# A retention layer and an FP4 feed-forward in one kernel: the old state read in two halves of 64 rows, the output projection behind the gate's projection, the gate product between the rotation's steps

## The chip, the cores and the metric

The kernel runs on one core of a Trainium2 chip. A core has TensorE (PE, matrix products; its weight loads are listed apart as PEld), VectorE (DVE), ScalarE (ACT), GpSimd (POOL) and a queue for DMAs (SP). Each works through its own list of instructions in order, and semaphores connect them. PE writes its results to PSUM, which has eight banks of 2 KB (512 fp32 numbers) in each of 128 partitions; DVE and ACT read them there. The metric is the device time of one execution in microseconds (us).

## What is computed

Input is x of shape (2, 2048, 256). First a retention layer (8 heads, 32 numbers of q and k and 64 of v in each), then a feed-forward whose activations and weights are rounded to FP4 in blocks of 16; behind both a residual and a layer norm.

```python
qkv = x @ w_qkv.T; q, k = xpos(q, k)            # a rotation by position
retention = einsum('bhtd,bhsd->bhts', q, k) * HD_QK**-0.5 * decay_mask   # causal, decay[h]**(t-s)
out = einsum('bhts,bhsv->bhtv', retention, v)
normed = (out - mean) / sqrt(var + eps)         # per head
y = (silu(x @ w_gated.T) * normed) @ w_proj.T
x = layernorm(x + y)
gate, up = fp4_linear(x, w_gate), fp4_linear(x, w_up)
x = layernorm(x + fp4_linear(silu(gate) * up, w_down))
```

The retention is computed in chunks of 128 positions: inside a chunk by scores, and what earlier chunks contribute by a running state of 32 x 64 per head, which decays from chunk to chunk.

## The kernel before

There are 32 tiles (16 chunks of 128 positions, two batches b that alternate, so tile n belongs to batch n % 2). All 32 go through the retention stage, with their results kept on the chip; then all go through the feed-forward. Every engine has a function `body(n, b, piece)` that writes out what it does around tile n of the first stage, and `both_loops` (L252) calls it: tiles -2 to 5 unrolled, tiles 6 to 29 in a loop of 12 rounds of two tiles (b = 0, then b = 1), tiles 30 and 31 unrolled. In the loop each round also quantises one piece of the feed-forward's weights (`w_max` to `w_exponent` on DVE, a rounding on ACT and three steps on POOL); the tile with b = 1 also quantises two finished tiles of x (`x_scale` to `x_exponent`). I call the tiles with b = 0 even and those with b = 1 odd.

There is no scheduler: the order of the calls in `body` is the order on the engine. For tile n it is

- PE (L1273): transposes of the rotated q and k (`turn_qk`, L1210), the projection of q and k of tile n+1 (L1178 into wide_banks), scores (L1221), transposes of the gated tile n-3 (L1261), the update of the state (`update`, L1250), the read of the old state (`cross`, L1230), the projection of v of tile n+1, the product of scores and v (`mix`, L1237), the output projection of tile n-3 (`project_out`, L1178 into upd_y), the projection of the gate of tile n+1 (`project_gate`).
- DVE (L804): the even tile has the root of nine variances as a chain of small steps (L675 to L720, its last result rstd at L715), the odd one the quantising. Both have `decay_q` (L617), `decay_scores` (L625), `split_gated` (L996), `sum_state` (L662), the rotation of tile n+1 (`rotate_products` L598 and L599, `rotate_sum` L609 and L610), in the even tile `w_max` (L759), then the gate product (`apply_gate`, L642), the residual of tile n-3 (`add_resid`, L632), its statistics (L636), the sums of squares (L648).
- ACT (L460): copies and activations; towards the end of a tile the eight scalings of the heads of tile n-2 (`normalise_heads`, L442), in the odd tile a rounding step of x (L404), a copy of v of tile n+1 (L424) and the squares of tile n (`square_heads`, L434).

`mixed`, one bank of 512 columns, takes first cross and then, added to it, mix. `cross` has two matmuls per tile, one per group of four heads: 128 rows of decayed q (4 heads x 32) against a block-diagonal state of 128 x 256, three quarters of it zero. Another bank, `upd_y`, holds the result of `update` (128 columns) and y, the result of `project_out` (256 columns).

`square_heads` reads mixed on ACT and `apply_gate` reads it on DVE; L639 makes DVE wait for the squares, so that the two don't read the bank together. `project_out` waits for `state_summed` of tile n (L1269), since DVE reads upd in y's bank. `add_resid` waits for `y_done`.

The semaphores that matter below: `squared` (ACT L434 to DVE L642), `opened_ready` (from L642), `y_done` (from project_out to DVE L632), `rot_ready` (from L610 to turn_qk), `ret_ready` (from L625 to the projection of v), `rstd_ready` (from L715 to ACT L442), and the step counter of the weights' quantising (from L778 to ACT L409).

## Time and profile before

| | us |
|---|---|
| median of three runs | 651.88 |
| lowest, highest | 650.33, 652.59 |
| the profiled execution | 651.12 |
| its span, first to last instruction | 649.3 |
| PE busy in the span | 583.6 (90%) |
| DVE busy | 552.7 (85%) |
| ACT busy | 337.6 (52%) |
| POOL busy | 230.9 (36%) |

The retention stage fills the span up to some 380 us, the feed-forward the rest. The loop over tiles 6 to 29 runs from about 95 to 354 us. Times in the trace's rows are microseconds from the start of the span. A busy PE is not a PE at its peak: matmuls are pipelined, their durations overlap, and so what a block of matmuls takes is read from its start to the start of the next block. On DVE and ACT too an instruction can start some 0.1 us before the one ahead of it has ended.

### The profile page before, as it was taken

What the parts mean: (1) busy time and instruction counts of PE and PEld (TensorE: products, weight loads), DVE (VectorE), ACT (ScalarE), POOL (GpSimd) and SP (SyncE); (2) the same over time, 40 slices, a digit from 0 to 9 for tenths busy, and PEclk for the clock granted to TensorE, in tenths of its full rate; (3) what the DMA queues carried; (4) which work ended last, traced back from release to release, by engine and by line L of the source; (5) the groups of instructions that cost most, each with busy time, mean ns of one, the idle gap of its engine ahead of it and who ended that gap; (6) DMA issues with size and microseconds to landing.
All of it is one profiled execution on the core that took longest, in us unless ns stands there. A gap on an engine that the chain in (4) does not pass through costs nothing. (4 is left out here: it accounts for less than half of the span.)

```text
span 649.3 us, 14685 instructions
## 1 busy us (share of the span) xinstructions
PE 583.6 (90%) x4290; PEld 498.6 (77%) x4290; DVE 552.7 (85%) x1439; ACT 337.6 (52%) x869; POOL 230.9 (36%) x262
## 2 busy tenths in 40 slices
PE   3269999999999999999999967786999999999975
PEld 2158888888888888888888856676999888888864
DVE  6047779999999999999999767887999999999996
ACT  3124666666756675667565654423454435444333
POOL 1011122344234523452344023435444444444430
PEclk9679999999999999999999979797999999999998
DMA  6471011101110111011101000000000000000001
GB/s 160 56 231 49 11 50 50 40 8 48 48 40 8 48 48 40 8 48 48 40 8 40 11 8 9 1 1 17 16 16 16 16 16 24 24 16 16 17 16 50
DMA packets 25853, 23.11 MB, mean 36 GB/s; under 512 B 2024, under 2 KB 22760, under 8 KB 25832
## 3 DMA queue, kind: packets, MB, share of 16 engines
q1 hardware_dynamic: 25016, 21.27, 11.6%
q10 hardware_dynamic: 816, 1.57, 0.7%
q8 instruction: 11, 0.18, 0.1%
q14 instruction: 10, 0.08, 0.0%
HBM read 17.56 MB, written 5.28 MB: 35 GB/s over the span
## 5 line engine op out<-in xcount | busy, mean ns | idle before, releaser
L1178 PE MATMUL wide_banks<-win_hi,x_hi 128*128 128x512 f32 x192 | 68.8, 440 | 12.9 <-DVE win_lo L882 11.0
L1154 POOL TENSOR_TENSOR shared<-shared,h_scale 128x704 f32<-128x704 bf16 x32 | 44.4, 1388 | 92.0 <-DVE shared L802 92.0
L1178 PE MATMUL wide_banks<-wgu_hi,xq_hi 128*128 128x512 f32 (+1 forms) x192 | 63.4, 413 | 10.6 <-DVE xq_lo L979 10.6
L442 ACT ACTIVATE shared<-opened,rstd 128x64 f32<-128x64 f32 x256 | 64.7, 335 | 11.4 <-DVE rstd L715 11.1
L413 ACT ACTIVATE shared<-shared 128x704 bf16<-128x704 f32 x32 | 25.3, 792 | 81.0 <-POOL shared L1149 81.0
L1237 PEld LDWEIGHTS mixed<-shared 128*128 128x128 f32 x512 | 62.0, 192 | 2.8
L1100 POOL TENSOR_TENSOR kd<-shared 128x128 f32<-128x128 f32 x60 | 23.2, 407 | 111.1 <-DVE shared L610 87.8
L1149 POOL TENSOR_TENSOR shared<-shared,h_inv 128x704 f32<-128x704 f32 x32 | 44.5, 1391 | 50.7 <-DVE h_inv L793 50.7
L1178 PE MATMUL wide_banks<-win_lo,x_hi 128*128 128x512 f32 x192 | 61.3, 401 | 0.0
L1178 PE MATMUL wide_banks<-win_hi,x_lo 128*128 128x512 f32 x192 | 60.9, 398 | 0.0
L1237 PE MATMUL mixed<-shared 128*128 128x64 f32 x512 | 60.6, 271 | 0.0
L1178 PE MATMUL wide_banks<-wgu_lo,xq_hi 128*128 128x512 f32 (+1 forms) x192 | 58.7, 388 | 0.0
L1178 PE MATMUL wide_banks<-wgu_hi,xq_lo 128*128 128x512 f32 (+1 forms) x192 | 57.7, 382 | 0.0
L1115 POOL TENSOR_TENSOR x_lo<-xf,x_hi 128x256 fp32r<-128x256 f32 x32 | 24.3, 758 | 87.5 <-ACT x_hi L394 87.5
L419 ACT ACTIVATE qkT<-turn 128x512 f32<-128x512 f32 x32 | 19.1, 598 | 57.6 <-PE turn L1210 57.6
L1178 PEld LDWEIGHTS wide_banks<-win_hi,x_hi 128*128 128x128 f32 x192 | 31.3, 194 | 19.6 <-issue 18.4
L1178 PEld LDWEIGHTS wide_banks<-wgu_hi,xq_hi 128*128 128x128 f32 x192 | 32.8, 198 | 15.2 <-DVE xq_lo L979 11.8
L1178 PEld LDWEIGHTS wide_banks<-win_lo,x_hi 128*128 128x128 f32 x192 | 37.1, 193 | 8.7
L1178 PEld LDWEIGHTS wide_banks<-win_hi,x_lo 128*128 128x128 f32 x192 | 36.6, 190 | 8.9
L625 DVE TENSOR_TENSOR shared<-wide_banks,shared 128x1024 f32<-128x1024 f32 x32 | 39.0, 1218 | 4.1 <-PE wide_banks L1221 4.1
L1178 PEld LDWEIGHTS wide_banks<-wgu_lo,xq_hi 128*128 128x128 f32 x192 | 37.2, 197 | 6.4
L1178 PEld LDWEIGHTS wide_banks<-wgu_hi,xq_lo 128*128 128x128 f32 x192 | 36.7, 193 | 6.3
(147 smaller groups left out, 1487.8 us busy)
## 6 DMA issues: line engine op xcount, KB each, us to landing
xf<-in_x_feat SPq DMA_DIRECT2D x32, 128.0 KB, 2.3
tab<-in_tables SPq DMA_DIRECT2D x16, 256.0 KB, 2.7
xt<-in_x_tok SPq DMA_DIRECT2D x32, 128.0 KB, 2.1
out<-shared SPq DMA_DIRECT2D x32, 128.0 KB, 1.7
x<-in_w_in ACTq DMA_DIRECT2D x3, 512.0 KB, 5.3
w<-in_w_gu SPq DMA_DIRECT2D x1, 1408.0 KB, 7.7
pow_dram<-powers SPq DMA_DIRECT2D x1, 1056.0 KB
w<-in_w_down SPq DMA_DIRECT2D x1, 704.0 KB, 9.0
```

The lines of the kernel that those rows point to most:

```text
L413: act.activation(h_size[:, b], h_unit[:, b], ACT.Abs, scale=SIZE_BY).then_inc(h_fp4["rounder_ready"], 1)
L419: act.activation(qkT[:].rearrange("p c t -> p (c t)"), turn[:], ACT.Copy).then_inc(qkT_ready, 1)
L442: last = act.activation(gated[:, b, cols], opened[:, b, cols], ACT.Copy, scale=rstd[:, b, 1 + k:2 + k])
L625: dve.tensor_tensor(ret[:].rearrange("p (j g) t -> p j (g t)", g=GROUPS), row_scores, dmask[:].rearrange("p (j g) t -> p j (g t)", g=GROUP ...
L1100: last = pool.tensor_tensor(kd[:, P * g:P * (g + 1)].rearrange("p (j d) -> p j d", d=DQ), rot[:, b, QK + P * g:QK + P * (g + 1)].rearrange ...
L1115: pool.tensor_tensor(x_lo[:, b], xf[:, b], x_hi[:, b].bitcast(F32), ALU.subtract).then_inc(x_lo_ready, 1)
L1149: pool.tensor_tensor(over_blocks(h_unit[:, b]), over_blocks(h), spread(h_fp4["inv"][:]), ALU.mult).then_inc(h_fp4["step"], 1)
L1154: pool.tensor_tensor(over_blocks(hq[:, b]), over_blocks(h_steps[:, b]), spread(h_fp4["scale"][:, b]), ALU.mult).then_inc(h_fp4["ready"], 1)
L1178: last = pe.matmul(dst, lhs, rhs, start=k == 0, stop=k == len(parts) - 1)
L1237: last = pe.matmul(mixed[:, DV * k:DV * (k + 1)], ret[:, slot(k)], vs[:, b, DV * k:DV * (k + 1)], start=False, stop=k == HEADS - 1, skip_g ...
```

## The change

Four things are changed together.

1. `cross` is split by rows: instead of two matmuls of 128 rows x 256 columns there are four of 64 rows x 128 columns. Rows 0 to 63 (heads j = 0, 1 of each group) write to one bank, rows 64 to 127 (j = 2, 3) to another. The block-diagonal state is 128 columns wide instead of 256. `mixed` is now the upper 256 columns of each of two banks, `mixed_banks`.
2. What was upd_y moves into the lower 256 columns of the same two banks: y into bank 0, upd into bank 1. Since banks are now shared otherwise, waits change: `update` and `project_out` wait for the gate product that read mixed (`opened_ready`), `cross` waits for `resid_done`, `mix` waits for `state_summed`. The signal that the update is done is given by `cross`, which stands behind it.
3. On PE `project_out` stands behind `project_gate` instead of ahead of it.
4. On DVE the gate product moves ahead: in the even tile between the second product of the rotation and its sums, in the odd tile between the first and the second product.

The heads' order in mixed, in the gate product and in the rows of w_proj is changed to suit (w_proj is loaded by two DMAs instead of one).

```diff
+def place(h):
+    g, j = divmod(h, PER)
+    return PER * (j // 2) + 2 * g + j % 2
...
-        mixed = psum("mixed", [P, BANK])
-        upd_y = psum("upd_y", [P, GROUPS * DV + DM])
-        upd = upd_y[:, 0:GROUPS * DV].rearrange("p (g v) -> p g v", v=DV)
-        y = upd_y[:, GROUPS * DV:]
+        mixed_banks = psum("mixed_banks", [P, 2, BANK])
+        mixed = mixed_banks[:, :, DM:BANK]
+        y = mixed_banks[:, 0, 0:DM]
+        upd = mixed_banks[:, 1, 0:GROUPS * DV].rearrange("p (g v) -> p g v", v=DV)
...
@@ the DMAs @@
-            sp.dma_start(wproj[:], w_proj.rearrange("(c p) n -> p c n", p=P)).then_inc(ld_proj, 16)
+            for r in range(2):
+                sp.dma_start(wproj[:, 2 * r:2 * r + 2], w_proj.rearrange("(g r p) n -> r p g n", g=GROUPS, p=P)[r]).then_inc(ld_proj, 16)
...
@@ ACT @@
-                act.activation(squares[:], mixed[:], ACT.Square, scale=DV ** -0.5).then_inc(squared, 1)
+                act.activation(halves(squares[:]), mixed, ACT.Square, scale=DV ** -0.5).then_inc(squared, 1)
...
-                    last = act.activation(state_bd[rows, b, :, DV * j:DV * (j + 1)], state[rows, b], ACT.Copy)
+                    last = act.activation(state_bd[rows, b, :, DV * (j % 2):DV * (j % 2 + 1)], state[rows, b], ACT.Copy)
...
@@ DVE @@
-                dve.tensor_tensor(opened[:, b], mixed[:], gate[:, b], ALU.mult).then_inc(opened_ready, 1)
+                dve.tensor_tensor(opened[:, b].rearrange("p (r g c) -> p r g c", r=2, g=GROUPS), mixed.rearrange("p r (g c) -> p r g c", g=GROUPS),
+                                  gate[:, b].rearrange("p (g r c) -> p r g c", g=GROUPS, r=2), ALU.mult).then_inc(opened_ready, 1)
...
                 if valid(n + 1):
-                    rotate_products(n + 1, 1 - b)
+                    rotate_cos(n + 1, 1 - b)
+                    if b == 0:
+                        rotate_sin(n + 1)
+                if valid(n):
+                    apply_gate(n, b)
+                if valid(n + 1):
+                    if b == 1:
+                        rotate_sin(n + 1)
                     rotate_sum(n + 1, 1 - b)
                 if w and b == 0:
                     w_max(piece)
-                if valid(n):
-                    apply_gate(n, b)
...
@@ PE, cross, mix, update, project_out @@
                 need(pe, opened_ready, n)
+                need(pe, resid_done, n - LAG)
                 for g in range(GROUPS):
-                    pe.matmul(mixed[:, PER * DV * g:PER * DV * (g + 1)], qdT[:, g], state_bd[:, b, g],
-                              start=g == 0, stop=False, skip_group_check=True)
+                    for r in range(2):
+                        rows = slice(2 * DQ * r, 2 * DQ * (r + 1))
+                        last = pe.matmul(mixed[:, r, 2 * DV * g:2 * DV * (g + 1)], qdT[rows, g], state_bd[rows, b, g],
+                                         start=g == 0, stop=False, skip_group_check=True)
+                if carried(n):
+                    last.then_inc(upd_done, 1)
...
                 pe.wait_ge(ret_ready, n + 1)
+                if carried(n):
+                    pe.wait_ge(state_summed, n + 1)
                 for k in range(HEADS):
...
-                need(pe, resid_done, n - LAG)
+                need(pe, opened_ready, n)
...
-                pe.wait_ge(state_summed, n + LAG + 1 if not isinstance(n, int) else min(n + LAG + 1, TILES - BATCH))
+                pe.wait_ge(opened_ready, n + LAG + 1 if not isinstance(n, int) else min(n + LAG + 1, TILES))
...
@@ PE, body @@
+                if valid(n + 1):
+                    project_gate(n + 1, 1 - b)
                 if in_turn(n - LAG):
                     project_out(n - LAG)
-                if valid(n + 1):
-                    project_gate(n + 1, 1 - b)
```

`project_out` is called with n - 3, so its new wait asks for the gate product of the tile whose mix stands just ahead of it.

How the orders read on the engines. PE of the kernel before, from mix to turn_qk of the next tile, with the semaphores that each first instruction waits for:

```order
L1237 MATMUL mixed<-shared 128x64 [waits ret_ready]
L1237 MATMUL mixed<-shared 128x64 x7
L1178 MATMUL upd_y<-wproj_hi,gatedT_hi 128x256 [waits state_summed,resid_done,gatedT_lo_ready]
L1178 MATMUL upd_y<-wproj_hi,gatedT_hi 128x256 x3
L1178 MATMUL upd_y<-wproj_lo,gatedT_hi 128x256 x4
L1178 MATMUL upd_y<-wproj_hi,gatedT_lo 128x256 x4
L1178 MATMUL wide_banks<-win_hi,x_hi 128x512 [waits ret_ready,gate_ready]
```

The same place in the changed kernel (L1264 is mix, L1197 is both projections, L1229 turn_qk):

```order
L1264 MATMUL mixed_banks<-shared 128x64 [waits state_summed,ret_ready]
L1264 MATMUL mixed_banks<-shared 128x64 x7
L1197 MATMUL wide_banks<-win_hi,x_hi 128x512 [waits ret_ready,gate_ready]
L1197 MATMUL wide_banks<-win_hi,x_hi 128x512
L1197 MATMUL wide_banks<-win_lo,x_hi 128x512 x2
L1197 MATMUL wide_banks<-win_hi,x_lo 128x512 x2
L1197 MATMUL mixed_banks<-wproj_hi,gatedT_hi 128x256 [waits opened_ready,resid_done,gatedT_lo_ready]
L1197 MATMUL mixed_banks<-wproj_hi,gatedT_hi 128x256 x3
L1197 MATMUL mixed_banks<-wproj_lo,gatedT_hi 128x256 x4
L1197 MATMUL mixed_banks<-wproj_hi,gatedT_lo 128x256 x4
L1229 MATMUL turn<-ident,shared 128x128 [waits gatedT_lo_ready,rot_ready]
```

The output projection has gone behind the gate's, and waits for the gate product of the same tile instead of the state's sum.

DVE in the loop's even tile, from the last steps of the roots to the residual, before:

```order
L715 SCALAR_TENSOR_TENSOR rstd<-poly,fine 128x18
L720 SCALAR_TENSOR_TENSOR shift<-moments,rstd 128x2
...
L598 TENSOR_TENSOR qk_cos<-wide_banks,tab 128x512
L599 TENSOR_TENSOR wide_banks<-wide_banks,tab 128x512
L609 TENSOR_TENSOR shared<-qk_cos,wide_banks 128x16x16
L610 TENSOR_TENSOR shared<-qk_cos,wide_banks 128x16x16
...
L759 TENSOR_REDUCE w_amax<-w 128x22
L642 TENSOR_TENSOR opened<-mixed,shared 128x512
...
L632 TENSOR_TENSOR resid<-upd_y,xt 128x256
```

and in the changed kernel (all line numbers are 10 to 14 higher there; L655 is the gate product, L645 the residual):

```order
L729 SCALAR_TENSOR_TENSOR rstd<-poly,fine 128x18
L734 SCALAR_TENSOR_TENSOR shift<-moments,rstd 128x2
...
L608 TENSOR_TENSOR qk_cos<-wide_banks,tab 128x512
L612 TENSOR_TENSOR wide_banks<-wide_banks,tab 128x512
L655 TENSOR_TENSOR opened<-mixed_banks,shared 128x512
L622 TENSOR_TENSOR shared<-qk_cos,wide_banks 128x16x16
L623 TENSOR_TENSOR shared<-qk_cos,wide_banks 128x16x16
...
L773 TENSOR_REDUCE w_amax<-w 128x22
...
L645 TENSOR_TENSOR resid<-mixed_banks,xt 128x256
```

The gate product has gone ahead of three instructions.

DVE in the odd tile of the changed kernel, with the waits:

```order
L766 TENSOR_SCALAR x_rounder<-x_unit 128x512 [waits x_step]
...
L608 TENSOR_TENSOR qk_cos<-wide_banks,tab 128x512 [waits rot_ready,ld_tab]
L655 TENSOR_TENSOR opened<-mixed_banks,shared 128x512 [waits gated_ready,gate_ready,squared]
L612 TENSOR_TENSOR wide_banks<-wide_banks,tab 128x512
L622 TENSOR_TENSOR shared<-qk_cos,wide_banks 128x16x16 [waits turned,kd_ready,sin_done,cos_done]
L623 TENSOR_TENSOR shared<-qk_cos,wide_banks 128x16x16
L643 ISA [waits y_done]
L645 TENSOR_TENSOR resid<-mixed_banks,xt 128x256 [waits x1_ready,ld_xt0]
```

Before, the gate product (L642, with the same waits) stood between L610 and the wait for y_done; three instructions of the rotation are now behind it. The order on ACT is as it was.

## Rows read from the trace of the kernel before

**Rows 1.** Engines between 100 and 200 us: busy us (instructions), clock, DMA; then waits.
```profile
100.00:200.00 100.00, 99.00 (x830) 82.27 (x830) 93.24 (x232) 66.18 (x191) 38.20 (x50) 1.00 0.13 40
...
PEld turn L1261 <- issue: 2.3, 12, 0.2
DVE opened L642 <- ACT squares L434: 1.9, 2, 1.2
```

**Rows 2.** Timeline of PE: start, us, engine, line, what; mix of an even tile onwards.
```profile
165.82 1.89 PE L1237 MATMUL mixed<-shared 128*128 128x64 f32 x16
167.52 0.71 PE L1178 MATMUL upd_y<-wproj_hi,gatedT_hi 128*128 128x256 f32 x4
...
169.02 0.62 PE L1178 MATMUL wide_banks<-win_hi,x_hi 128*128 128x512 f32 x2
...
170.42 0.60 PE L1210 MATMUL turn<-ident,shared 128*128 128x128 f32 x4
...
181.44 0.60 PE L1210 MATMUL turn<-ident,shared 128*128 128x128 f32 x4
```

**Rows 3.** Timeline of DVE in the same even tile.
```profile
161.93 0.75 DVE L694 SCALAR_TENSOR_TENSOR fine<-rsq,root 128x18 f32<-128x18 f32 x1
...
165.51 0.18 DVE L715 SCALAR_TENSOR_TENSOR rstd<-poly,fine 128x18 f32<-128x18 f32 x1 [0.20 <-DVE poly L709]
...
166.67 0.69 DVE L599 TENSOR_TENSOR wide_banks<-wide_banks,tab 128x512 f32<-128x512 f32 x1
...
168.12 0.51 DVE L759 TENSOR_REDUCE w_amax<-w 128x22 f32 x1
...
168.74 0.69 DVE L642 TENSOR_TENSOR opened<-mixed,shared 128x512 f32<-128x512 f32 x1
...
169.41 0.42 DVE L632 TENSOR_TENSOR resid<-upd_y,xt 128x256 f32<-128x256 f32 x1
```

**Rows 4.** Timeline of ACT in the same even tile.
```profile
165.72 2.02 ACT L442 ACTIVATE shared<-opened,rstd 128x64 f32<-128x64 f32 x8 [0.71 <-DVE rstd L715]
...
168.13 0.58 ACT L434 ACTIVATE squares<-mixed 128x512 f32<-128x512 f32 x1
```

**Rows 5.** Timeline of DVE, PE and ACT in the odd tile that follows.
```profile
173.74 0.34 DVE L778 TENSOR_SCALAR w_rounder<-w_unit 128x352 uint32<-128x352 uint32 x1
174.00 1.22 DVE L625 TENSOR_TENSOR shared<-wide_banks,shared 128x1024 f32<-128x1024 f32 x1
...
174.11 0.50 ACT L409 ACTIVATE w_rounder<-w_rounder 128x352 f32<-128x352 f32 x1 [1.67 <-DVE w_rounder L778]
...
175.36 0.70 PE L1178 MATMUL wide_banks<-win_hi,x_hi 128*128 128x512 f32 x2 [0.15 <-DVE shared L625]
...
178.05 0.68 DVE L598 TENSOR_TENSOR qk_cos<-wide_banks,tab 128x512 f32<-128x512 f32 x1
...
179.23 0.59 ACT L434 ACTIVATE squares<-mixed 128x512 f32<-128x512 f32 x1
...
180.09 0.69 DVE L642 TENSOR_TENSOR opened<-mixed,shared 128x512 f32<-128x512 f32 x1
...
180.69 0.41 DVE L632 TENSOR_TENSOR resid<-upd_y,xt 128x256 f32<-128x256 f32 x1
```

**Rows 6.** One tile's scores and cross: durations in ns, first and last start in us.
```profile
L1221 PE MATMUL wide_banks<-qkT x16: 270/270/372, 183.4 to 183.9; 32*128 32x128 f32 x16
...
L1230 PE MATMUL mixed<-shared,qdT x4: 379/379/483, 185.0 to 185.8; 128*128 128x256 f32 x4
```

**Rows 7.** Timeline of the first tiles: gate product and turn_qk; output projection, gate product, residual.
```profile
53.97 0.69 DVE L642 TENSOR_TENSOR opened<-mixed,shared 128x512 f32<-128x512 f32 x1 [1.75 <-ACT squares L434]
...
54.59 0.60 PE L1210 MATMUL turn<-ident,shared 128*128 128x128 f32 x4
...
71.03 0.72 PE L1178 MATMUL upd_y<-wproj_hi,gatedT_hi 128*128 128x256 f32 x4
...
71.89 0.69 DVE L642 TENSOR_TENSOR opened<-mixed,shared 128x512 f32<-128x512 f32 x1 [1.43 <-ACT squares L434]
...
72.74 0.42 DVE L632 TENSOR_TENSOR resid<-upd_y,xt 128x256 f32<-128x256 f32 x1 [0.15 <-PE upd_y L1178]
```

28 lines of the change are left out of this document (16 added, 12 removed).

## The prediction, made before the changed kernel had run

> **What bounds the kernel now.** I read the table of engines by stretch first. Between 100 and 200 us, inside the loop, PE is busy 99.0 us of 100, and it is tempting to stop there: PE is the limit, and cross, which multiplies by three quarters of zeros, is PE time to save. But DVE is busy 93.2 us of the same 100 [rows 1], with most of the rest being the short gaps between small steps that depend on each other. So the second thing to read is who waits for whom. From 100 us to the stage's end the gate product was held up by ACT's squares only twice, 1.9 us together [rows 1], while PE, once a round, stands for DVE's decayed scores ahead of the projection of v: they end at 174.00 + 1.22 = 175.22, and the projection starts at 175.36 with a wait of 0.15 before it [rows 5]. DVE waits for practically nobody and PE waits a little for DVE. **In the loop DVE sets the pace, with PE just behind.** In the tiles ahead of the loop, where no weights are quantised, it is the reverse: the gate product stands 1.75 and 1.43 us in wait for the squares [rows 7], and PE sets the pace.
>
> Third, the timelines, for what lies around the gate product. Even tile: rstd is ready at 165.69 [rows 3]; ACT starts its eight scalings at 165.72, goes on without a gap, and its squares run from 168.13 to 168.71 [rows 4]; the gate product starts at 168.74 [rows 3]. So from rstd to the gate product there is a fixed chain on ACT of 168.74 - 165.69 = **3.05 us**, and before the change DVE fills just this time: shift, both products of the rotation, its two sums and the weights' maxima, the last ending at 168.12 + 0.51 = 168.63 [rows 3]. Odd tile: ACT is released by DVE's L778 at 173.74 + 0.34 = 174.08, starts at 174.11 and is busy until the squares end at 179.23 + 0.59 = 179.82 [rows 5]. This chain takes **5.77 us** to 179.85, when a gate product could begin; DVE begins it at 180.09, having come from the rotation's sums. Neither chain starts earlier or gets shorter by the change.
>
> **The change part by part.**
>
> *The gate product moved ahead, even tile.* Only shift and the two products are left to fill the 3.05 us. They end at 166.67 + 0.69 = 167.36 [rows 3], so DVE stands from then until 168.74: 1.4 us idle, which before were the sums and the maxima. The gate product ends at 169.43, as now. The two sums and the maxima then follow in some 1.1 us (before, they filled 167.36 to 168.63, with 0.1 us of latencies), up to 170.53.
>
> *The output projection behind the gate's, waiting for the gate product.* Before, it started at 167.52 and was followed at 169.02 by the gate's projection, 1.50 us later; that one takes 170.42 - 169.02 = 1.40 us [rows 2]. Now the gate's projection runs from 167.52 to 168.92, and the output projection waits for the gate product, 169.43. A wait from DVE to PE costs 0.14 us (175.22 to 175.36 [rows 5]), so it starts at 169.57. From its start to the residual's start go 72.74 - 71.03 = 1.71 us [rows 7]. The residual therefore starts at 169.43 + 0.14 + 1.71 = 171.28, against 169.41 before [rows 3]: **1.87 us later**, with DVE idle for 0.8 of them. DVE is in order, so all that it has queued behind the residual is 1.87 us late: the statistics, the sums of squares, the x and weight steps and, at the end of the row, the decayed scores for which PE waits.
>
> *Odd tile.* Counted from the odd tile's own start, the first product ends at 178.05 + 0.68 = 178.73 [rows 5]. The gate product cannot start before 179.85; it ends at 180.54, the output projection starts at 180.68 and the residual at 180.54 + 1.85 = 182.39, against 180.69 before [rows 5]: **1.70 us later**. Second product (0.69) and sums (some 0.85) fit into this wait. PE's turn_qk would be ready at 180.68 + 1.50 = 182.18, where it stood at 181.44 [rows 2]; rot_ready, at some 182.0, is in time. So nothing that PE does between is late; PE merely comes to the next wait for DVE earlier and stands there.
>
> A round of two tiles thus costs 1.87 + 1.70 = 3.57 us more, and since both anchors (rstd and L778) are DVE's own and move with it, nothing is won back in the next round: 12 x 3.57 = **42.8 us**.
>
> *Cross in halves.* Scores are the nearest thing in the trace: groups of rows of 32 in separate banks. 16 passes of 128 columns start within 183.4 to 183.9, four abreast in four rounds, and cross has its four passes of 256 columns at 185.0 to 185.8 [rows 6]. The new cross has eight passes of 128 columns, two abreast: also four rounds, so some 0.5 for 0.8, 0.3 us less, if they overlap; if they don't, as long as before. The array then changes its shape once more per tile; the change after scores shows 2.3 us in 12 cases, 0.2 each [rows 1]. I take 0.15 us less per tile, between 0.3 less and 0.2 more. In the loop PE waits for DVE anyway, so this gives nothing there. In the six tiles ahead of it: -0.9 us, between -1.8 and +1.2. The Trainium skill (TensorEngine Tiling (Array Packing), Theoretical Speedup and Key Properties) gives up to twice the speed at 64 rows or fewer, and says that changing the mode drains the array. By that the cross would save half of its 0.8 us, 0.4 in each tile, less a drain that the page does not price; by the rows it is 0.15.
>
> *Ahead of the loop.* Tiles 0 to 2 have no output projection that could cover the later rotation. In tile 1 (odd) the gate product ends at 54.66; then second product and sums, as in the odd tile above about 1.45 us, and 0.15 to PE: turn_qk at 56.26 instead of 54.59 [rows 7], 1.7 us late. In tiles 0 and 2 (even) only the sums are behind it, 0.75: by the same account 0.9 each. In tiles 3 to 5 the output projection ends 0.14 + 1.50 after the gate product: tile 3 at 71.89 + 0.69 + 1.64 = 74.22, where turn_qk stood at 71.03 + 1.50 + 1.40 = 73.93 [rows 2, 7]; 0.3 late, and 0.4 in tile 4. In tile 5 the residual's 1.7 us counts in full, less some 0.45 that DVE still had in hand on entering the loop. Together 0.9 + 1.7 + 0.9 + 0.3 + 0.4 + 1.7 - 0.45 = 5.4, less 0.9 for cross: **+4.5 us**.
>
> *Behind the loop.* Tiles 30 and 31: output projection behind the gate product, 0.4 in tile 30, less 0.3 of a wait of DVE for scores that is there now; in tile 31 a residual that holds up a group of the turned weights by 0.7: **+0.8 us** as an estimate, and up to 3 if all of the groups behind it are held up.
>
> *What costs nothing.* The new waits of mix (for sum_state, which ends about 1 us after the decayed scores, while PE has the v projection of some 1.5 us ahead of mix), of cross and update (for results of the tile before), the two DMAs of w_proj (at the start, not needed until tile 3), the wider views of squares and gate product (the same 512 numbers). If the views were 10% slower, 0.13 us per tile in the chain, 3 us over the loop; I keep that for the range.
>
> *Given back.* L694 takes 0.75 us at 161.93 in place of the 0.18 of its like, L715 [rows 3]; GpSimd's split of x runs beside it. PE, which releases that split, will run about a microsecond further ahead of DVE, so the collision moves to other steps. Between 0 and 0.6 us per round; I take 0.3, as it may meet another small step: **-3.6 us**, between -7 and 0.
>
> Sum: 42.8 + 4.5 + 0.8 - 3.6 = +44.5 us. From the profiled execution's 651.12 us (0.8 below the median of 651.88) that is 695.6, and on the median 696.4. I say **696 us**.
>
> **The rivals.**
>
> *Only the move on DVE bites.* If the output projection came in time for the residual (were y_done not to wait for the gate product plus 1.71), the even tile would lose 1.1 us (sums and maxima behind the gate product) and the odd one 1.2 us (180.54 to the end of product and sums): 12 x 2.3 = 28, with the ends about 680. Against it: the wait for the same tile's gate product stands in the order on PE, and 1.71 us is a row, not a guess.
>
> *PE's saving comes through: faster.* One mechanism: if PE and not DVE paced the loop, the shorter cross would shorten each tile, and the gate product would be released early enough since mix ends earlier. Price: 32 x 0.3 = 9.6 us off, 641.5. (By the rule of the skill's tiling page, 32 x 0.4, it would be 638.) It decides from the point where DVE's idle time per round is more than what the gate product's new place costs, 3.6 us. DVE has 6.8 us idle in 100, 1.5 a round, even counting its latencies [rows 1]. Against it also: the squares don't follow mix's end but ACT's scalings, which follow rstd [rows 4].
>
> *The waits cost more than counted.* PE now stands for some 3.5 us in a round of 25; if the granted clock fell to 1.2 GHz in such places, as nothing inside this loop shows so far (it is 1.00 [rows 1]), or if the collision with GpSimd grows, it is 710 or more.
>
> *The change does not do what it says*, that is, the old waits already were as late as the new ones, and the time stays within 0.3%, some 651: the row with only two waits for the squares speaks against it [rows 1].
>
> **How the numbers follow.** The forecast, both waits in force, 0.75; only the move bites, 0.10; more than counted, 0.08; no change, 0.02; PE's saving comes through, 0.05. The forecast's own range: from -7 for the collision and -1 for cross to +3 for the views and +2 for the end, 690 to 702. To hold 8 in 10 with what I may have missed in following two tiles I take it down to the first rival: 680 to 704. A measurement of this kernel can tell a difference of about 0.3% (2 us). Slower by more than that holds in the first three cases, 0.93; same 0.02; faster 0.05.
>
> **What the profile of the changed kernel would show.** The gate product in the loop with an idle time before it, waiting for squares: 1.4 us in even tiles, 1.1 in odd ones. The residual with an idle time before it, waiting for PE's output projection: 0.8 and 0.3. A round of some 25 us between turn_qk and turn_qk two tiles on, where it was 21.6. PE waiting for DVE's decayed scores ahead of the projection of v by 1 to 2 us in each tile. DVE's busy share in the loop down from 93% to some 80 to 82%. Four rounds of cross in about 0.5 us. The feed-forward as long as before. I am wrong if the gate product starts without a wait, or if the loop's round stays near 21.6 us.

## The result, and the profile after

The changed kernel takes 704.79 us (median of 4 runs, 702.09 to 708.20), against 651.63 us for the kernel before: **1.082 times as long, interval 1.0754 to 1.0886**. The forecast was 696 us, its range 680 to 704. The direction is right; the loss of 53 us is some 20% larger than the 44.5 forecast and lies just outside the range. The runs stand in two groups, two at 702.09 and two at 707.49 and 708.20; the former had a mean granted clock of 0.964, the latter of 0.957 and 0.954, and what that has to do with the times is taken up below. The profiled execution is one of the latter (708.20, its span 706.4).

First the engines of the whole span and TensorE's clock in 40 slices, then the table by stretch for 100 to 200 us (us in the stretch, busy time and instructions of PE, PEld, DVE, ACT and POOL, clock, share of DMA, GB/s), which answers the first of [rows 1]:

```profile
PE 593.4 (84%) x4418; PEld 500.4 (71%) x4418; DVE 548.5 (78%) x1439; ACT 337.6 (48%) x869; POOL 231.7 (33%) x262
...
PEclk9679999999999999999999997999999999999997
```
```profile
100.00:200.00 100.00, 86.27 (x751) 70.31 (x752) 78.65 (x199) 56.43 (x160) 32.15 (x43) 0.98 0.11 32
```

Outside of the stretches at half clock (1.2 GHz instead of 2.4) no instruction got longer in a way that matters, and only PE has more of them (128 more passes of cross). In the loop both engines now stand: PE went from 99.0 to 86.3 us of 100, DVE from 93.2 to 78.7. What they stand for is in the table of waits, 100 to 440 us (who waits for whom: us in all, times, longest):

```profile
DVE opened L655 <- ACT squares L442: 38.0, 26, 2.3
...
PE turn L1287 <- DVE qdT L630: 26.0, 26, 1.4
...
DVE resid L645 <- PE mixed_banks L1197: 20.8, 27, 1.2
...
PE mixed_banks L1197 <- DVE opened L655: 13.1, 21, 2.2
...
PE wide_banks L1197 <- DVE shared L638: 7.4, 24, 0.6
```

Before, the first of these waits came twice with 1.9 us in all [rows 1]; now it comes 26 times, once in each tile of the stretch. The timeline shows the place, an odd tile (the first two rows) and the even one behind it:

```profile
200.10 0.69 DVE L655 TENSOR_TENSOR opened<-mixed_banks,shared 128x512 f32<-128x512 f32 x1 [1.13 <-ACT squares L442]
...
202.82 0.42 DVE L645 TENSOR_TENSOR resid<-mixed_banks,xt 128x256 f32<-128x256 f32 x1 [0.57 <-PE mixed_banks L1197]
...
209.00 0.18 DVE L729 SCALAR_TENSOR_TENSOR rstd<-poly,fine 128x18 f32<-128x18 f32 x1 [0.20 <-DVE poly L723]
...
210.17 0.69 DVE L612 TENSOR_TENSOR wide_banks<-wide_banks,tab 128x512 f32<-128x512 f32 x1
...
211.62 0.58 ACT L442 ACTIVATE squares<-mixed_banks 128x512 f32<-128x512 f32 x1
...
212.23 0.69 DVE L655 TENSOR_TENSOR opened<-mixed_banks,shared 128x512 f32<-128x512 f32 x1 [1.38 <-ACT squares L442]
...
213.07 0.71 PE L1197 MATMUL mixed_banks<-wproj_hi,gatedT_hi 128*128 128x256 f32 x4 [0.59 <-DVE opened L655]
...
214.57 0.60 PE L1229 MATMUL turn<-ident,shared 128*128 128x128 f32 x4
...
214.96 0.42 DVE L645 TENSOR_TENSOR resid<-mixed_banks,xt 128x256 f32<-128x256 f32 x1 [0.94 <-PE mixed_banks L1197]
```

From the end of rstd (209.18) to the gate product are 3.05 us, as in [rows 3, 4]. DVE's second product ends at 210.86; the sums and the maxima that used to fill the rest now stand behind the gate product, so DVE is idle for 1.38 us. Then the output projection starts 0.15 after the gate product's end at 212.92, and the residual 1.89 after its start at 213.07. Before, the residual started 0.67 us after the gate product's start [rows 3].

### The profile page after: what moved, and what is told of

It reads as the page before. It is cut to its first block, busy times and chain, and to the rows that moved or that the text cites. A ratio compares the mean times of both kernels' runs of the same rounds, so it can differ in the third digit from the quotient of the medians.

```text
span 706.4 us, 14991 instructions
## 1 busy us (share of the span) xinstructions
PE 593.4 (84%) x4418; PEld 500.4 (71%) x4418; DVE 548.5 (78%) x1439; ACT 337.6 (48%) x869; POOL 231.7 (33%) x262
## 4 chain that ended last, share of the span: by engine, by line
DVE 35%; PE 20%; issue 19%; POOL 7%; ACT 7%; DVEq 2%; ACTq 0%; POOLq 0%
PE mixed_banks L1197 8%; PE wide_banks L1197 6%; PE mixed_banks L1264 4%; POOL shared L1168 4%; ACT shared L450 3%; POOL shared L1173 3%; DVE shared L811 2%; DVE shared L638 2%; DVE opened L655 2%; DVE shared L816 2%; ACT squares L442 2%; DVE stats L649 2%; DVE h_amax L796 2%; DVE resid L645 2%; DVE shared L1009 1%
## 5 line engine op out<-in xcount | busy, mean ns | idle before, releaser
L1197 PE MATMUL wide_banks<-win_hi,x_hi 128*128 128x512 f32 x192 | 71.3, 454 | 19.4 <-DVE win_lo L901 10.9
L1173 POOL TENSOR_TENSOR shared<-shared,h_scale 128x704 f32<-128x704 bf16 x32 | 44.5, 1392 | 92.0 <-DVE shared L816 89.6
L1197 PE MATMUL wide_banks<-wgu_hi,xq_hi 128*128 128x512 f32 (+1 forms) x192 | 62.2, 406 | 10.2 <-DVE xq_lo L998 10.2
L1264 PEld LDWEIGHTS mixed_banks<-shared 128*128 128x128 f32 x512 | 65.3, 199 | 3.3
L1197 PE MATMUL wide_banks<-win_lo,x_hi 128*128 128x512 f32 x192 | 63.7, 414 | 0.0
L1197 PE MATMUL wide_banks<-win_hi,x_lo 128*128 128x512 f32 x192 | 63.5, 413 | 0.0
L655 DVE TENSOR_TENSOR opened<-mixed_banks,shared 128x512 f32<-128x512 f32 x32 | 22.1, 692 | 53.2 <-ACT squares L442 53.2
L1264 PE MATMUL mixed_banks<-shared 128*128 128x64 f32 x512 | 63.1, 278 | 0.0
L1168 POOL TENSOR_TENSOR shared<-shared,h_inv 128x704 f32<-128x704 f32 x32 | 44.5, 1392 | 49.8 <-DVE h_inv L807 49.8
L1197 PE MATMUL wide_banks<-wgu_lo,xq_hi 128*128 128x512 f32 (+1 forms) x192 | 58.3, 386 | 0.0
L1197 PE MATMUL wide_banks<-wgu_hi,xq_lo 128*128 128x512 f32 (+1 forms) x192 | 58.2, 385 | 0.0
L1197 PEld LDWEIGHTS wide_banks<-win_hi,x_hi 128*128 128x128 f32 x192 | 30.5, 199 | 24.8 <-issue 24.2
L1287 PE MATMUL turn<-ident,shared 128*128 128x128 f32 x128 | 21.0, 289 | 31.5 <-DVE qdT L630 27.6
L1197 PEld LDWEIGHTS wide_banks<-win_hi,x_lo 128*128 128x128 f32 x192 | 38.3, 200 | 9.6
L1197 PEld LDWEIGHTS wide_banks<-win_lo,x_hi 128*128 128x128 f32 x192 | 38.3, 200 | 9.2
L1197 PEld LDWEIGHTS wide_banks<-wgu_hi,xq_hi 128*128 128x128 f32 x192 | 32.2, 194 | 15.2 <-DVE xq_lo L998 11.0
L1197 PEld LDWEIGHTS wide_banks<-wgu_hi,xq_lo 128*128 128x128 f32 x192 | 36.8, 194 | 6.1
```

What stands on the lines that cost most here:

```text
L655: dve.tensor_tensor(opened[:, b].rearrange("p (r g c) -> p r g c", r=2, g=GROUPS), mixed.rearrange("p r (g c) -> p r g c", g=GROUPS), gate ...
L1168: pool.tensor_tensor(over_blocks(h_unit[:, b]), over_blocks(h), spread(h_fp4["inv"][:]), ALU.mult).then_inc(h_fp4["step"], 1)
L1173: pool.tensor_tensor(over_blocks(hq[:, b]), over_blocks(h_steps[:, b]), spread(h_fp4["scale"][:, b]), ALU.mult).then_inc(h_fp4["ready"], 1)
L1197: last = pe.matmul(dst, lhs, rhs, start=k == 0, stop=k == len(parts) - 1)
L1264: last = pe.matmul(mixed[:, r, DV * at:DV * (at + 1)], ret[:, slot(k)], vs[:, b, DV * k:DV * (k + 1)], start=False, stop=k >= HEADS - 2, s ...
L1287: last = pe.transpose(turn[:, P * c:P * (c + 1)], gated[:, b, P * c:P * (c + 1)], ident[:])
```

## The experiments

All times are medians with their range; a ratio is against the kernel before, run on the same chip. "Round" is the time of two tiles in the loop, from one transposition of q and k in an even tile to that of the next; it is the sharper measure. Before it is 21.60 us, after it is 25.10 in undisturbed rounds: **+3.50**.

**One part at a time.** The change has three parts in the loop: DVE's gate product earlier, PE's output projection later, and the projection's wait for the gate product, which the shared bank of y and mixed calls for. Each of them alone was put into the kernel before, and the first was taken out of the kernel after.

The gate product early, nothing else:
```diff
@@ DVE, the body of a tile @@
                 if valid(n + 1):
-                    rotate_products(n + 1, 1 - b)
+                    rotate_cos(n + 1, 1 - b)
+                    if b == 0:
+                        rotate_sin(n + 1)
+                if valid(n):
+                    apply_gate(n, b)
+                if valid(n + 1):
+                    if b == 1:
+                        rotate_sin(n + 1)
                     rotate_sum(n + 1, 1 - b)
                 if w and b == 0:
                     w_max(piece)
-                if valid(n):
-                    apply_gate(n, b)
```


> The kernel before with only DVE's order changed as in the change (gate product between the rotation's steps). Theory: DVE waits for the squares 1.4 and 1.1 us, the residual is 1.1 and 1.2 us late, round 23.6 to 23.9 us; tiles 0 to 2 3.5 us longer; 679 us (674 to 684). Rival (the place on DVE carries all of the loss): 695 to 705 us.

Measured 680.06 us (678.68 to 680.62), ratio 1.0437 (1.0408 to 1.0467); the round 23.63, +2.03. As expected.

The output projection late, nothing else:
```diff
@@ PE, the body of a tile @@
-                if in_turn(n - LAG):
-                    project_out(n - LAG)
                 if valid(n + 1):
                     project_gate(n + 1, 1 - b)
+                if in_turn(n - LAG):
+                    project_out(n - LAG)
```


> The kernel before with only PE's order changed: output projection behind the gate's projection, without the wait for the gate product. Theory: the residual waits for y, which comes 1.40 us later: 1.22 us late in the even tile (167.52 + 1.40 + 1.71 = 170.63 against 169.41) and 0.93 in the odd one, 0.3 given back, round 23.4 us, 674 us (669 to 680). Rival (PE sets the pace, the order of two projections is neutral): 651 us.

Measured 679.19 us (677.83 to 679.23), ratio 1.0424 (1.0395 to 1.0454), at the upper end of what was expected; the round 23.53, +1.93. The waits of its 100 to 340 us say where: the residual stands for the output projection in nearly every tile.
```profile
DVE resid L632 <- PE upd_y L1178: 23.3, 20, 1.7
```

The wait alone, in both old orders:
```diff
@@ project_out @@
                 need(pe, resid_done, n)
...
+                pe.wait_ge(opened_ready, n + LAG + 1 if not isinstance(n, int) else min(n + LAG + 1, TILES))
```


> The kernel before with one more wait: the output projection also waits for the gate product of the same tile (opened_ready). All orders are as before. Theory (the wait of the output projection for the gate product sets the loop, since the residual stands behind both on DVE): residual 1.87 us late in the even tile (169.43 + 1.85 against 169.41), 1.94 in the odd one (180.78 + 1.85 against 180.69), 0.4 for scores that now come late, 0.3 given back: a round of some 25.5 us instead of 21.6, and tiles 3 to 5 1.7 us longer each; in all 704 us (700 to 710). Rival (the gate product's earlier place on DVE is what costs): this wait ends at a time at which the residual was due anyway, under 660 us.

Measured **735.57 us** (732.68 to 738.72), ratio 1.1308 (1.1255 to 1.136): the wait alone costs more than the whole change. This missed by 30 us. The round is 27.3. An undisturbed and a disturbed output projection of the kernel with the wait alone, in that order:
```profile
211.46 0.71 PE L1178 MATMUL upd_y<-wproj_hi,gatedT_hi 128*128 128x256 f32 x4 [2.18 <-DVE opened L642]
...
213.33 0.42 DVE L632 TENSOR_TENSOR resid<-upd_y,xt 128x256 f32<-128x256 f32 x1 [2.02 <-PE upd_y L1178]
...
224.02 1.20 PE L1178 MATMUL upd_y<-wproj_hi,gatedT_hi 128*128 128x256 f32 x4 [1.82 <-DVE opened L642]
...
226.72 0.76 PE L1178 MATMUL wide_banks<-win_hi,x_hi 128*128 128x512 f32 x2
...
227.15 0.42 DVE L632 TENSOR_TENSOR resid<-upd_y,xt 128x256 f32<-128x256 f32 x1 [3.27 <-PE upd_y L1178]
```
```profile
223.30:226.70 3.40, 2.68 (x12) 2.71 (x13) 0.57 (x1) 0.84 (x2) 0.20 (x1) 0.54 0.29 95
```
Two things add. PE, in order, has the gate's projection and the transposition of q and k queued behind the waiting output projection, so 2 us of PE's time are lost in every tile, and DVE in its turn stands 2 us at the residual. And once in each round the granted clock is at its lower level (0.54 in the stretch of the last row, where 0.5 is 1.2 GHz) just when the output projection runs: its 12 matmuls go from 224.02 to 226.72, 2.7 us, where they take 1.51 at 2.4 GHz (211.46 to 212.97). That is 1.2 of the 5.7 us added; without it the round would be some 26, an estimate, which is still 4.5 us more than before. The expectation had 3.9 for the wait and nothing for the clock; it also had tiles 3 to 5 longer by 1.7 us each, and they are longer by 3.2 to 3.4.

The kernel after with the old order on DVE (the first diff, reversed):


> The changed kernel with DVE's order put back to that of before (gate product behind the rotation's sums and the weights' maxima). Theory (wait of the output projection): nothing is won in the loop, since the gate product ends at the same time in even tiles and 0.24 later in odd ones, round 25.1 to 25.4; tiles 0 to 2 get their 3.5 us back; 699 to 706 us. Rival (the gate product's place carries the loss): 20 us or more faster than the changed kernel, 680 us.

Measured 704.68 us (702.97 to 705.69), ratio 1.0814 (1.0782 to 1.0846); the round 25.32 against 25.10. So with the wait in force it is all but equal where the gate product stands. As expected.

The parts don't add: 2.03 and 1.93 alone, and 5.7 (about 4.5 at full clock) for the wait alone, yet 3.50 for all three. Between the kernel with the wait alone and the last one lie 735.57 - 704.68 = 31 us. The two differ by the output projection's place and by the halves with their banks, and the halves by themselves are worth some 5 us (below). So most of the 31 us is the move: it makes the wait bearable, and it is a loss without it.

**Halves without the wait.** If the wait is the cause and not the narrower cross, the halves must do no harm once y has a place of its own. Columns 256 to 511 of the first bank of scores are free from the decayed scores to the next tile's scores. For all tiles but the last three, the output projection writes there, and the residual reads it there:
```diff
+        y_early = score[:, 0, DM:BANK]
+        y_of = lambda n: y if isinstance(n, int) and n >= TILES - LAG else y_early
...
@@ scores @@
+                need(pe, resid_done, n - LAG)
@@ cross @@
-                need(pe, resid_done, n - LAG)
@@ project_out @@
-                pe.wait_ge(opened_ready, n + LAG + 1 if not isinstance(n, int) else min(n + LAG + 1, TILES))
+                if isinstance(n, int) and n >= TILES - LAG:
+                    pe.wait_ge(opened_ready, TILES)
+                pe.wait_ge(ret_ready, n + LAG + 1 if not isinstance(n, int) else min(n + LAG + 1, TILES))
```
with both old orders:


> The halves alone: the changed kernel with y in the upper half of a score bank (free there in the retention stage), so that the output projection does not wait for the gate product; both orders (PE and DVE) as in the kernel before. Scores wait for the residual that read y, which is done 2 us earlier. Theory (DVE paces the loop, so cheaper cross gives nothing there): round 21.6 us, tiles 0 to 5 and 30, 31 some 0.15 us shorter each, 650 us (648 to 652). Rival 1 (PE paces the loop): round 21.0 us, 641 us. Rival 2 (the halves themselves cost, by the change of shape): 655 us or more.

with both new orders:


> The changed kernel with all its orders, but y in the upper half of a score bank, so that the output projection does not wait for the gate product. Theory: the wait falls away, both moves stay: residual 1.2 us late in each tile, 23.7 to 24.0 us a round, tiles 0 to 2 3 us longer, 682 us (677 to 688). Rival (the wait never mattered): 702 us or more.

with PE's new order and DVE's old one:


> As the kernel with y in a score bank, and DVE's order put back; only the output projection stands behind the gate's, and cross is in halves. Theory: as the kernel before with PE's order alone (679 us, round 23.53), less 1 to 2 us for cross ahead of the loop: 677 us (674 to 680), round 23.3 to 23.5.

| y in the scores' bank | us | ratio | round |
|---|---|---|---|
| both old orders | 646.71 (645.97 to 647.69) | 0.993 (0.9913 to 0.9946) | 21.30 |
| both new orders | 684.69 (683.48 to 685.05) | 1.0504 (1.0482 to 1.0527) | 23.82 |
| only PE's new order | 681.09 (678.77 to 681.83) | 1.0443 (1.0418 to 1.0468) | 23.54 |

The halves alone make the kernel **0.7% faster**; what makes the change slow is the output projection's later place (+2.2 a round by itself, +2.5 together with DVE's move) and, on top, the wait (+1.3: 23.82 to 25.10). The second line of the table is as expected. The first is a miss by 3 us, to the better, and lies between the theory (650) and the rival in which PE sets the pace (641). The third is a miss by 4 us, to the worse, though its round is nearly what was expected (23.3 to 23.5). The halves gave nothing there (23.54 against 23.53 for the same order with the whole cross), and its loop has four stretches at half clock, the first two at 113 and 161 us, so that the clock of its 100 to 200 us is 0.97 (the third figure from the end):
```profile
100.00:200.00 100.00, 88.99 (x787) 74.31 (x785) 82.37 (x209) 58.45 (x166) 33.83 (x44) 0.97 0.11 32
```
The four rounds with such a stretch took 24.7 to 25.1 us, some 5 us more in all.

The stretch from 100 to 200 us, first of the halves with both old orders, then of those with both new ones, where the clock stays at 1.00:
```profile
100.00:200.00 100.00, 96.75 (x878) 81.61 (x877) 93.39 (x233) 67.42 (x192) 39.60 (x51) 1.00 0.14 40
```
```profile
100.00:200.00 100.00, 88.30 (x809) 73.14 (x809) 84.27 (x214) 58.32 (x165) 35.35 (x47) 1.00 0.11 32
```
In tiles 3 to 5, which PE paces, a tile takes 10.28 us where it took 10.54: **cross in halves saves 0.26 us of PE per tile**, the further change of the array's shape included. In the loop it saves 0.15 per tile, where I had counted nothing.

**Who paces the loop of before.** That last number contradicts "in the loop DVE sets the pace": if it did, a shorter cross would give nothing. So the same question was put from DVE's side. One product of 128x512 whose result nothing uses goes in ahead of the weights' maxima of the even tile, in the kernel before:
```diff
                 if w and b == 0:
+                    flat_cos = qk_cos[:].rearrange("p w o j -> p (w o j)")
+                    dve.tensor_tensor(probe[:], flat_cos, flat_cos, ALU.mult)
                     w_max(piece)
```


> A probe: the kernel before with one product of 128x512 more per round on DVE (0.69 us, 0.61 of its own, result unused), ahead of the weights' maxima in the even tile. Theory (DVE paces the loop): the gate product moves by 0.5 to 0.6 us, the round from 21.6 to 22.15, 658 us (656 to 660). Rival (PE paces it): 651 to 652 us.

and the same in the kernel after, behind the second product, ahead of the waiting gate product:


> The same probe in the changed kernel, between the second product of the rotation and the gate product, where DVE is expected to stand idle 1.4 us for the squares in even tiles. Theory: it costs nothing there, 702 to 708 us as without it. Rival (DVE's work and not its waits sets the changed kernel's time): 7 us more, 710 to 715 us.

In the kernel before: 652.15 us (650.96 to 652.85, 10 runs), ratio 1.0007 (0.9995 to 1.0018); the round 21.66 to 21.75. A miss: 0.6 us more of DVE's work per round cost 0.1, not 0.55. The time is the rival's (PE sets the pace), but the rival's ground is not what the rows show: PE alone needs 21.13 (below). Four rows of its timeline say what gave way:
```profile
161.86 0.77 POOL L1118 TENSOR_TENSOR x_lo<-xf,x_hi 128x256 fp32r<-128x256 f32 x1 [1.03 <-ACT x_hi L395]
161.86 0.18 DVE L695 SCALAR_TENSOR_TENSOR fine<-rsq,root 128x18 f32<-128x18 f32 x1
162.07 0.59 DVE L701 TENSOR_TENSOR rsq<-fine 128x18 f32<-128x18 f32 x1
...
173.10 0.51 DVE L775 TENSOR_TENSOR w_unit<-w,w_inv 128x352 f32<-128x352 f32 x1
```
The step that took 0.75 us in [rows 3] beside GpSimd's split of x (there L694) is down to 0.18, while another, L701, has gone from 0.18 to 0.59 and ends when the split does (162.66 and 162.63); w_unit went from 0.71 to 0.51. The collision moved to shorter encounters, and from the residual to the decayed scores DVE needs 0.16 us less in an even tile and 0.21 less in an odd one. Another 0.11 went into idle time that stood ahead of the gate product. The Trainium skill (SBUF — State Buffer, Who interferes with whom) says that a DVE instruction with two inputs in SBUF and a GpSimd instruction that reads SBUF exclude one another, and that the order of issue decides which one waits; the rows agree for the two small steps, 0.75 and 0.59 us in place of 0.18.

In the kernel after the probe costs nothing in a round: 25.09 to 25.10. Its total is 708.50 us (707.89 to 709.23), ratio 1.0883 (1.0864 to 1.0903), the level of after's longer runs, with four stretches at half clock in the loop of its profiled execution. So the idle time ahead of the gate product is real: 0.6 us of work fits into it free of charge.

**A version that beats both.** If PE and DVE are close, both have to be relieved. To the halves with both old orders was added: the product w_unit (0.71 us of DVE, beside GpSimd) goes to GpSimd, which is busy 38 us in 100 [rows 1], and w_scale and w_inverse move from the odd tile to the end of the even one:
```diff
@@ DVE, the body of a tile @@
                 if in_turn(n - LAG):
                     add_resid(n - LAG, 1 - b)
+                if w and b == 0:
+                    w_scale(piece)
+                if in_turn(n - LAG):
                     resid_stats(n - LAG, 1 - b)
+                if w and b == 0:
+                    w_inverse(piece)
...
-                    w_unit(piece)
@@ GpSimd, the body of a tile @@
                 if carried(n):
                     decay_k(n, b)
+                if piece is not None and b == 1:
+                    pool.wait_ge(w_fp4["step"], FP4_STEPS * piece + 3)
...
+                                       spread(w_fp4["inv"][:]), ALU.mult).then_inc(w_fp4["step"], 1)
```


> The halves alone (y in a score bank, old orders), and in the loop one step of the weights' quantising, the product with the inverse (128x352, 0.71 us on DVE, 0.6 of its own), moved from DVE to GpSimd; DVE takes scale and inverse of the weights at the end of the even tile instead of the odd one. Theory (DVE paces the loop, and behind it PE waits for it 0.5 to 0.65 us a round): round 20.7 us instead of 21.3, 640 us (638 to 643). Rival (PE's own work is the limit at 21.3): 646 to 647 us.

and the same move in the kernel before, without the halves:


> The kernel before with the same step moved from DVE to GpSimd and nothing else. Theory: PE is only 0.15 to 0.3 us a round behind DVE there, so the round goes from 21.6 to 21.3 us and PE becomes the limit: 648 us (647 to 650). Rival (PE's full cross is no limit): 644 us.

| | us | ratio | round |
|---|---|---|---|
| halves, w_unit on GpSimd | **638.75** (638.37 to 639.40) | 0.981 (0.9796 to 0.9825) | 20.67 |
| before, w_unit on GpSimd | 644.35 (643.94 to 646.40) | 0.9905 (0.9884 to 0.9927) | 21.13 |

The first is 1.9% faster than the kernel before, and its 100 to 200 us show why it goes no further: PE has nothing left to wait for.
```profile
100.00:200.00 100.00, 99.68 (x904) 83.79 (x903) 94.03 (x237) 68.56 (x195) 45.88 (x60) 1.00 0.14 40
```
The second is a miss: expected were 648 us and a round of 21.3, and the time is the rival's (644). The rival's ground, that PE's full cross is no limit, fails all the same, since PE is busy 99.95 us of 100 there. 21.13 is what PE needs for a round with the whole cross: tiles 3 to 5 of before, at 10.54 each, had said so all along (21.1 for two). So in the kernel before, DVE's pace (21.60) and PE's (21.13) lie 0.47 us apart. A shorter cross (0.5 off PE a round) brought 0.30, more work for DVE brought 0.1, and less work for DVE brought the whole 0.47. DVE's pace is not a fixed number either: it gives where GpSimd's instructions fall otherwise.

## Why the prediction was right or wrong

**Right, and near in size.** The gate product moved ahead meets a chain on ACT that does not start earlier. Forecast waits 1.4 (even) and 1.1 (odd), measured 1.38 and 1.13. The residual waits for the output projection: forecast 0.8 and 0.3, measured 0.94 and 0.57. A round of "some 25 us": 25.10. DVE's share "80 to 82%" is just under (78.65 us of 100), and the feed-forward is as long as before. PE does wait for DVE in each tile, but the place was named wrongly: 26.0 us of it stand ahead of the transposition of the gated values, behind qdT (L1287), and only 7.4 ahead of the projection of v. That had no price in the sum.

**Wrong in size.** The direction and both waits held. What failed are terms of the sum: the clock, which was priced at nothing (measured +5.3 us); the residual behind the output projection, 0.38 us a round too short (+4.6); tiles 4 and 5 (+2.7); and the end (+1.6). More was given back than forecast (-1.8). The sum was +44.5 on the profiled execution's own time; its span grew by 706.4 - 649.3 = 57.1. By the terms, reading the residual's start of tile 5, of the loop's last tile and of the last tile of all:

| term | forecast | measured |
|---|---|---|
| ahead of the loop | +4.5 | +7.75 (93.84 to 101.59) |
| loop, the residual later, 12 rounds | +42.8 (3.57 each) | +47.4 (3.95 each) |
| given back | -3.6 (0.30 each) | -5.4 (0.45 each) |
| loop, half clock | 0 | +5.3 |
| loop, sum | +39.2 | +46.8 (259.65 to 306.49) |
| behind the loop | +0.8 | +2.4 |

(47.4 - 5.4 + 5.3 is 47.3; the 0.45 over are the first round of the loop before, which took 22.02.) Where each term failed:

*Ahead of the loop: +3.2, most of it in tiles 4 and 5.* Of the 3.2, 0.57 arose before tile 0's transposition of q and k (17.62 for 17.05) and 2.7 in tiles 4 and 5. Tiles 0 to 2 came out as reckoned (0.52, 1.63 and 0.84 against 0.75, 1.55 and 0.75), tile 3 too (0.15). But I let tile 4 be late only by what the output projection does to PE, 0.25, on the ground that PE paces it, and gave tile 5 with the residual 1.1 in all. Before, tile 4 took 10.54 us and tile 5 10.56; after, 11.99 and 11.76, and the residual of tile 5 stands another 1.39 later against the transposition that follows tile 5. Kernel after, then kernel before, the beginning of tile 4:
```profile
77.64 0.60 PE L1229 MATMUL turn<-ident,shared 128*128 128x128 f32 x4
77.84 0.42 DVE L645 TENSOR_TENSOR resid<-mixed_banks,xt 128x256 f32<-128x256 f32 x1 [0.40 <-PE mixed_banks L1197]
...
81.47 1.22 DVE L638 TENSOR_TENSOR shared<-wide_banks,shared 128x1024 f32<-128x1024 f32 x1
...
89.63 0.60 PE L1229 MATMUL turn<-ident,shared 128*128 128x128 f32 x4
```
```profile
73.93 0.60 PE L1210 MATMUL turn<-ident,shared 128*128 128x128 f32 x4
...
76.71 1.21 DVE L625 TENSOR_TENSOR shared<-wide_banks,shared 128x1024 f32<-128x1024 f32 x1
```
The residual now comes behind the transposition of q and k, where before it stood 1.2 us ahead of it (72.74 [rows 7] and 73.93), and DVE's queue behind it is so long that the decayed scores start 3.83 us after the transposition instead of 2.78. A change that holds up DVE by over a microsecond turns a stretch that PE paces into one that DVE paces; I had used the pacing of before for the kernel after.

*The residual: 3.95 a round for 3.57.* In both tiles the gate product starts as far behind its anchor as forecast (3.05 and 5.77 us). Short was the piece behind it: 1.71 us from the output projection's start to the residual's, taken from tile 3 of before [rows 7], where it is 1.89 and 1.88 here. So from rstd to the residual go 5.78 us instead of 3.72 (3.68 in every other round) [rows 3], and from the end of w_rounder (L792, before L778) 8.49 instead of 6.61 [rows 5]. Why the piece is longer than in tile 3 is open.

*Given back: 0.45 a round, where 0.30 was taken.* The stretches in which DVE works through its queue, from the residual to the next anchor, got shorter: 202.82 to 209.18 is 6.36 where it was 6.62, and 189.85 to 194.33 is 4.48 where it was 4.67. The rows of the odd tile after, and the residual ahead of the even tile before:
```profile
189.85 0.42 DVE L645 TENSOR_TENSOR resid<-mixed_banks,xt 128x256 f32<-128x256 f32 x1 [0.95 <-PE mixed_banks L1197]
...
193.37 0.51 DVE L788 TENSOR_TENSOR w_unit<-w,w_inv 128x352 f32<-128x352 f32 x1
193.99 0.34 DVE L792 TENSOR_SCALAR w_rounder<-w_unit 128x352 uint32<-128x352 uint32 x1
```
```profile
159.07 0.41 DVE L632 TENSOR_TENSOR resid<-upd_y,xt 128x256 f32<-128x256 f32 x1
```
In the odd tile w_unit takes 0.51 us for 0.71. In the even tile the step of 0.75 us (L694) is down to 0.18, but another (L693, before L679) is up from 0.18 to 0.58 (204.76 to 205.34) beside GpSimd's split of x, which ends at 205.31: the collision moved, as in the probe above. The round, +3.50, is 3.95 less 0.45. It lies near the 3.57 of the first reckoning only because these two errors run against each other; net of the 0.3, the forecast was 3.27.

*Half clock: +5.3, priced at nothing and given a chance of 0.08 as a rival.* Once at 119 us, and from 221 us on in every second round, there is a stretch in which the records show TensorE at its lower level, 1.2 GHz. The table by stretch of two rounds after each other, and of 3 us within the second:
```profile
177.34:202.45 25.11, 21.34 (x190) 17.33 (x189) 19.87 (x50) 14.10 (x40) 8.51 (x12) 1.00 0.11 31
202.45:228.68 26.23, 22.89 (x191) 18.65 (x190) 19.87 (x50) 14.21 (x40) 8.48 (x12) 0.93 0.10 30
...
217.50:220.00 2.50, 1.30 (x26) 1.07 (x28) 2.39 (x10) 0.53 (x2) 0.00 (x0) 1.00 0.36 105
...
221.00:224.00 3.00, 3.00 (x11) 2.50 (x10) 2.90 (x6) 2.96 (x11) 1.96 (x2) 0.51 0.00 0
```
DVE, ACT and GpSimd do the same work in both rounds; PE is busy for 1.55 us more and the round is 1.12 longer. In the stretch ahead of the fall PE was busy 1.30 us of 2.50; it stood 1.43 for DVE's qdT, up to 218.70. But the round ahead of it has that wait too, and keeps its clock; what decides between the two the rows don't show. There are five such stretches in the loop, each 3.4 us long. Before, the clock in the loop was 1.00 [rows 1]. The two runs at 702.09 us, whose mean clock is 0.964, lie 50.5 us above before, which fits a loop nearly free of such stretches. Only a longer run has a profile; that this one mechanism makes the 6 us between the groups is likely and not shown.

*Cross* was worth 0.26 us per tile where PE paces, not the 0.15 taken (the range was 0.3 less to 0.2 more). The Trainium skill's factor of up to two (TensorEngine Tiling (Array Packing), Theoretical Speedup and Key Properties) would have been 0.4 less a drain that it doesn't price; measured is 0.26 net. And "in the loop PE waits for DVE anyway, so this gives nothing there" was wrong by 0.30 us a round, as the halves alone show. In the kernel after it most likely gives nothing; that was not tested by itself, but with only PE's order changed the round is 23.54 with the halves and 23.53 without.

**The rivals.** "Only the move on DVE bites" (680) is out: taking that move back changes nothing (704.68), and alone it gives 680.06, just the number that the rival had. "PE's saving comes through" had a true core (0.7%) that the halves alone show, but its point of decision, an idle time of 3.6 us on DVE, is not reached. "More than counted" is what happened in part.

**The range.** Its upper end, 702 and then 704, left out what the working itself allowed: nothing given back (+3.6). With that, the views and the end it would have been some 705, and the 704.79 inside; by luck, since what came is the clock, the residual and tiles 4 and 5.

**Shown and not shown.** Shown by taking parts away: the wait (20 us: 704.79 to 684.69, of which 4 to 5 are stretches at half clock, since that kernel's loop has a single one, in its last round) and the two moves (38 us: 684.69 to 646.71). Shown by rows only: the residual's 1.89, tiles 4 and 5, and the half clock, whose cause stays open. The 2.4 us behind the loop was not taken apart.

## What to carry to other kernels

- Moving a consumer ahead on its engine gives nothing if what it waits for hangs on a fixed chain from that same engine (here 3.05 us from rstd over ACT): the filling work comes out behind it, and everything queued after is late. Look for the anchor first.
- A bank or buffer that two tensors share is paid for with waits between their readers and writers. Here that wait cost 1.3 us a round behind a reordering that was itself a loss, and 5.7 without it (1.2 of them by the clock); a free half of another bank made it vanish, and with the old orders the packing became a gain.
- Two engines within some 2% of each other have no single "bound". Each part of the loop that only one of them paces (here tiles 3 to 5) shows the other's limit, and a change must relieve both.

## What the runs showed of the hardware that I had not expected

- The clock in the loop is 1.00 with PE busy 99 us of 100 [rows 1]. Five stretches of 3.4 us at 1.2 GHz, some 1.1 us each, stand in the loop after (PE busy 86 of 100 there), one in nearly every round with the wait alone (85), four with y in the scores' bank and only PE's order new (89), one with only PE's order new in the kernel before (91, at 325 us). The loop with y in the scores' bank and both orders new (88) has a single one, in its last round, and the one with the gate product early (93) none. So waits of 1 to 2 us in every tile can cost more than themselves, but PE's busy share does not say in which of these kernels they do. It matters too what PE is doing when the clock falls.
- A collision of a small DVE step with GpSimd (0.75 for 0.18 us) is no fixed charge: work added on DVE moved it and cost a sixth of its own length.
- Cross on halves of the rows, kernel before and kernel after:
```profile
185.02 1.13 PE L1230 MATMUL mixed<-shared,qdT 128*128 128x256 f32 x4
```
```profile
219.62 0.72 PE L1252 MATMUL mixed_banks<-shared,qdT 64*128 64x128 f32 x8
```
Twice the passes, two abreast, take 0.41 us less by these durations, but durations of passes overlap. From the first pass of cross to the projection of v are 0.78 us in tile 4 of the kernel before (77.51 to 78.29) and 0.65 with the halves alone (77.50 to 78.15), and the whole tile is 0.26 shorter. What the further change of the array's shape costs, no row shows by itself.
